# Cross-scan layers: the softplus's difference from GpSimd to VectorE, without ScalarE's pass that subtracts the one

## What is computed

```python
delta = jax.nn.softplus(delta + delta_bias[None, :, None])
def step(h, inp):
    dt, ut, bt, ct = inp
    dA = jnp.exp(dt[..., None] * A_k[None])
    dBu = dt[..., None] * bt[:, :, None, :] * ut[..., None]
    h = dA * h + dBu
    y = jnp.einsum('bkdn,bkn->bkd', h, ct)
    return (h, y)
```

## Time and profile before

| what | us |
|---|---|
| median of 3 runs | 3782.1 |
| fastest and slowest run | 3761.59 and 3788.62 |
| span of the profiled execution | 3763.2 |
| one image of the last layer, order-0 turn and order-1 turn | 182.4 and 169.2 |

### The profile page before, as it was taken

How to read it: one execution, slowest core, us unless ns; L and a number is a source line. 1 busy time by engine, 2 the same in 40 slices (tenths; PEclk the granted TensorE clock), 3 DMA queues, 4 the chain that set the end, 5 groups by cost and what they waited for, 6 DMA issues and landing times. The chain is left out here.

```text
span 3763.2 us, 27831 instructions
## 1 busy us (share of the span) xinstructions
PE 2803.9 (75%) x6084; PEld 631.1 (17%) x6084; DVE 3005.3 (80%) x1944; ACT 2039.5 (54%) x2278; POOL 2826.3 (75%) x1212
## 2 busy tenths in 40 slices
PE   5668777877887788345667677688878787877887
PEld 2111111111111111111111121111111111111111
DVE  1889898888889896676988824988889888889883
ACT  3566565656565664314555425656565556656562
POOL 1899899988999897003655515999889989989993
PEclk9788888778788878667889788778787878888788
DMA  2655646553755554103443305475555555564652
GB/s 59 156 124 137 147 124 159 127 132 98 164 129 140 126 142 101 28 2 89 119 102 86 100 3 124 108 168 131 130 125 136 136 126 136 134 139 122 156 126 56
DMA packets 140402, 437.16 MB, mean 116 GB/s; under 512 B 33429, under 2 KB 34139, under 8 KB 139915
## 3 DMA queue, kind: packets, MB, share of 16 engines
q1 hardware_dynamic: 140234, 435.53, 48.2%
HBM read 307.50 MB, written 6.82 MB: 84 GB/s over the span
## 5 line engine op out<-in xcount | busy, mean ns | idle before, releaser
L863 POOL TENSOR_TENSOR L_read<-L_state,L_c_rows 128x1024 f32<-128x1024 f32 x768 | 1800.6, 2363 | 206.7 <-PE L_y_ps L656 176.7
L656 PE MATMUL L_y_ps<-L_read,L_fold 128*64 128x512 f32 x3072 | 1256.5, 913 | 426.2 <-POOL L_read L863 390.0
L794 ACT ACTIVATE L_work_ps<-L_delta,L_a_neg 128x1024 f32<-128x1024 f32 x256 | 286.3, 1118 | 677.2 <-DVE L_state L971 677.2
L971 DVE TENSOR_TENSOR_SCAN L_state<-L_work_ps,L_state 128x1024 f32<-128x1024 f32 x256 | 583.7, 2280 | 80.4 <-POOL L_state L850 76.6
L850 POOL TENSOR_TENSOR L_state<-L_du,L_b_rows 128x1024 f32<-128x1024 f32 x256 | 606.0, 2367 | 25.1 <-POOL L_read L863 3.1
L971 DVE TENSOR_TENSOR_SCAN L_state<-L_decay,L_work_ps 128x1024 f32<-128x1024 f32 x256 | 585.3, 2286 | 29.9 <-DVE L_work_ps L952 6.8
L794 ACT ACTIVATE L_decay<-L_delta,L_a_neg 128x1024 f32<-128x1024 f32 x512 | 584.9, 1142 | 14.6 <-DVE L_state L971 11.3
L971 DVE TENSOR_TENSOR_SCAN L_state<-L_decay,L_row_ps 128x1024 f32<-128x1024 f32 x256 | 585.5, 2287 | 8.8
L952 DVE TENSOR_TENSOR L_work_ps<-L_du,L_row_ps 128x1024 f32<-128x1024 f32 x256 | 314.4, 1228 | 268.5 <-issue 143.2
L656 PEld LDWEIGHTS L_y_ps<-L_read,L_fold 128*64 128x64 f32 x3072 | 184.9, 159 | 1372.8 <-POOL L_read L863 976.4
L1501 POOL TENSOR_TENSOR L_read<-L_state,L_c_rows 128x1024 f32<-128x1024 f32 x96 | 235.5, 2458 | 189.7 <-PE L_y_ps L1297 106.4
(11 more groups left out here) (322 smaller groups left out, 2981.1 us busy)
## 6 DMA issues: line engine op xcount, KB each, us to landing
L_c_rows<-L_bc_dram SPq DMA_DIRECT2D x580, 256.0 KB, 4.0
L_b_rows<-L_bc_dram SPq DMA_DIRECT2D x580, 256.0 KB, 4.2
L_delta<-L_delta SPq DMA_DIRECT2D x204, 256.0 KB, 5.9
L_du<-L_du SPq DMA_DIRECT2D x140, 256.0 KB, 6.2
L_du<-L_u SPq DMA_DIRECT2D x64, 256.0 KB, 6.0
L_bc_dram<-L_dbl SPq DMA_DIRECT2D x40, 128.0 KB, 3.5
L_delta<-L_delta_a SPq DMA_DIRECT2D x16, 256.0 KB, 4.4
L_du<-L_du_a SPq DMA_DIRECT2D x16, 256.0 KB, 5.3
```

Of the source, the lines that this page charges most:

```text
L656: m = nc.tensor.matmul(y_ps[i * BLK:(i + 1) * BLK, c, :], fold[:, :], y_half(t, o, i), start=first, stop=last, skip_group_check=True)
L794: nc.scalar.activation(to[:, :], delta2[:, d * NBLK + c, :], ACT.Exp, scale=a_neg[:, o * 2 + d, c, p:p + 1]).then_inc(decay_ready, 1)
L863: nc.gpsimd.tensor_tensor(read[:, t % READS, :], state[:, t % STATES, :], c_rows[:, g % 2, :], ALU.mult).then_inc(multiplied, 1)
L971: nc.vector.tensor_tensor_scan(state[:, c, way], by[:, way], fed[:, way], 0.0, ALU.mult, ALU.add).then_inc(scanned, 1)
```

## The change

The gap moves from GpSimd's list to VectorE's. It is now one instruction that takes the rounded sum `more` = 1 + e as it is, adds -1 and subtracts l; ScalarE's "less" and its constant column go away, and the gap waits for "one" instead. A new table puts the gaps behind VectorE's scans of tiles 30, 38 and 41 in order 0 and of tiles 23, 29 and 35 in order 1. In the head, VectorE makes the three gaps before its first tile, and GpSimd forms du only. The conv-scan layer stays as it was.

```diff
-POOL_GAP = [{29: 0, 36: 1, 39: 2}, {22: 0, 28: 1, 34: 2}]
+DVE_GAP = [{30: 0, 38: 1, 41: 2}, {23: 0, 29: 1, 35: 2}]
...
                     if j > 0 or not isinstance(turn, Head):
                         act.wait_ge(sp_gap, n)
                     nc.scalar.activation(more[:, :], e[:, :], ACT.Identity, bias=1.0).then_inc(sp_one, 1)
-                elif kind == "less":
-                    act.wait_ge(sp_one, n + 1)
-                    nc.scalar.activation(more[:, :], more[:, :], ACT.Identity, bias=minus_col[:, :]).then_inc(sp_less, 1)
                 else:
                     act.wait_ge(sp_gap, n + 1)
                     nc.scalar.activation(l[:, :], l[:, :], ACT.Relu).then_inc(sp_relu, 1)
...
                         if at == t:
                             softplus(turn, kind, j)
 
-            ahead = {0: (("exp", 0), ("log", 0), ("one", 0), ("less", 0), ("exp", 1), ("log", 1), ("relu", 0), ("one", 1),
-                         ("less", 1)),
-                     1: (("exp", 2), ("log", 2), ("relu", 1), ("one", 2), ("less", 2)), 2: (("relu", 2),)}
+            ahead = {0: (("exp", 0), ("log", 0), ("one", 0), ("exp", 1), ("log", 1), ("relu", 0), ("one", 1)),
+                     1: (("exp", 2), ("log", 2), ("relu", 1), ("one", 2)), 2: (("relu", 2),)}
             for _, key, i in HEAD_SIDES:
                 if key[0] == "sum" and i == 0:
                     for kind, j in ahead[key[1]]:
...
 
         @block.gpsimd
         def _(pool):
-            def gap(turn, j):
-                n = turn.next * NJ + j
-                pool.wait_ge(sp_log, n + 1)
-                pool.wait_ge(sp_less, n + 1)
-                l = l_of[j]
-                nc.gpsimd.tensor_tensor(l[:, :], more[:, :], l[:, :], ALU.subtract).then_inc(sp_gap, 1)
-
             def add_x(turn):
 
                 wait_side(pool, turn.use(("out", 0), 1))
...
                                             ALU.mult).then_inc(multiplied, 1)
                     if turn.finish and t == ADD_AT:
                         add_x(turn)
-                    if t in POOL_GAP[turn.r]:
-                        gap(turn, POOL_GAP[turn.r][t])
 
             def form_du(j):
 
                 wait_side(pool, Head().use(("sum", j), 1))
                 nc.gpsimd.tensor_tensor(du[j], delta[:, j, :], u[:, j, :], ALU.mult).then_inc(sp_du, 1)
 
-            gap(Head(), 0)
-            gap(Head(), 1)
-            form_du(0)
-            gap(Head(), 2)
-            form_du(1)
-            form_du(2)
+            for j in range(NJ):
+                form_du(j)
             over_turns(pool, turn_of)
             add_x(Tail())
 
...
                     dve.wait_ge(rooted, done + 1)
                     nc.vector.tensor_tensor(sq_b[0:C, s], sq_a[0:C, s], side_ps[0:C, :], ALU.mult).then_inc(side_free, 1)
 
+            def gap(turn, j):
+
+                n = turn.next * NJ + j
+                dve.wait_ge(sp_log, n + 1)
+                dve.wait_ge(sp_one, n + 1)
+                l = l_of[j]
+                nc.vector.scalar_tensor_tensor(out=l[:, :], in0=more[:, :], scalar=-1.0, in1=l[:, :], op0=ALU.add,
+                                               op1=ALU.subtract).then_inc(sp_gap, 1)
+
             def inject_tile(number, t):
 
                 T, (d, p, c) = number * NT + t, tiles[t]
...
                     way = slice(None, None, 1 if d == 0 else -1)
                     nc.vector.tensor_tensor_scan(state[:, c, way], by[:, way], fed[:, way], 0.0, ALU.mult,
                                                  ALU.add).then_inc(scanned, 1)
-
+                    if t in DVE_GAP[turn.r]:
+                        gap(turn, DVE_GAP[turn.r][t])
+
+            for j in range(NJ):
+                gap(Head(), j)
             over_turns(dve, turn_of)
             for _, key, i in TAIL_SIDES:
                 if key[0] in ("cent", "shift", "out"):
```

More of the change, by code:

```diff
@@ L319 @@
             ("dt", 2): (22, 24), ("u", 2): (26, 27), ("sum", 0): (28, 29), ("sum", 1): (31, 32), ("sum", 2): (36, 37)}]
-ACT_SOFTPLUS = [{("exp", 0): 28, ("log", 0): 29, ("one", 0): 30, ("less", 0): 31, ("relu", 0): 33, ("exp", 1): 36,
-                 ("log", 1): 37, ("one", 1): 38, ("less", 1): 39, ("exp", 2): 39, ("log", 2): 40, ("relu", 1): 41,
-                 ("one", 2): 41, ("less", 2): 42, ("relu", 2): 44},
-                {("exp", 0): 21, ("log", 0): 22, ("one", 0): 23, ("less", 0): 24, ("relu", 0): 26, ("exp", 1): 27,
-                 ("log", 1): 28, ("one", 1): 29, ("less", 1): 30, ("relu", 1): 32, ("exp", 2): 33, ("log", 2): 34,
-                 ("one", 2): 35, ("less", 2): 36, ("relu", 2): 38}]
-POOL_GAP = [{29: 0, 36: 1, 39: 2}, {22: 0, 28: 1, 34: 2}]
+ACT_SOFTPLUS = [{("exp", 0): 28, ("log", 0): 29, ("one", 0): 30, ("relu", 0): 33, ("exp", 1): 36,
+                 ("log", 1): 37, ("one", 1): 38, ("exp", 2): 39, ("log", 2): 40, ("relu", 1): 41,
+                 ("one", 2): 41, ("relu", 2): 44},
+                {("exp", 0): 21, ("log", 0): 22, ("one", 0): 23, ("relu", 0): 26, ("exp", 1): 27,
+                 ("log", 1): 28, ("one", 1): 29, ("relu", 1): 32, ("exp", 2): 33, ("log", 2): 34,
+                 ("one", 2): 35, ("relu", 2): 38}]
+DVE_GAP = [{30: 0, 38: 1, 41: 2}, {23: 0, 29: 1, 35: 2}]
 ACT_SIDES = ("u", "bc", "dt", "sum", "z", "cent", "var")
@@ L410, in cross_scan_layer @@
         eps_col = sb("eps_col", [128, 1])
-        minus_col = sb("minus_col", [128, 1])
         w_u, w_z, w_bc_a, w_bc_b, w_dt = given.w_u, given.w_z, given.w_bc_a, given.w_bc_b, given.w_dt
@@ L439, in cross_scan_layer @@
         (set_up, consts, side_ready, side_free, sp_abs, sp_exp, sp_log, sp_one,
-         sp_less, sp_gap, sp_relu, sp_du, delta_ready, decay_ready, scanned, injected, injected_c, b_ready,
+         sp_gap, sp_relu, sp_du, delta_ready, decay_ready, scanned, injected, injected_c, b_ready,
          multiplied, y_added, bc_stored, y_free, y_out, rooted, silued, gated, x_added) = (
@@ L443, in cross_scan_layer @@
                 "set_up", "consts", "side_ready", "side_free", "sp_abs", "sp_exp", "sp_log",
-                "sp_one", "sp_less", "sp_gap", "sp_relu", "sp_du", "delta_ready", "decay_ready",
+                "sp_one", "sp_gap", "sp_relu", "sp_du", "delta_ready", "decay_ready",
                 "scanned", "injected", "injected_c", "b_ready", "multiplied", "y_added", "bc_stored", "y_free", "y_out", "rooted",
@@ L501, in cross_scan_layer @@
         tiles = [(d, p, c) for d in range(DIRS) for p in range(NP) for c in range(NBLK)]
-        n_setup = 4 + 1 + 2 + 4 + 4 + 2
+        n_setup = 3 + 1 + 2 + 4 + 4 + 2
         @block.sync
@@ L900, in _ @@
             setup(nc.vector.memset(eps_col[:, :], eps))
-            setup(nc.vector.memset(minus_col[:, :], -1.0))
             setup(nc.vector.tensor_tensor(fold[:, :], ident[:, 0:BLK], ident[:, BLK:128], ALU.add))
```

## The result

The changed kernel takes 3752.4 us, the kernel before 3772.7 (medians of 20 runs each). The ratio is 0.9944, 95% interval 0.993 to 0.9959: 20 us or 0.56% faster, inside the 1% that the prediction called the limit of a measurement, and inside its range. The median of three runs from which the forecast subtracted its 16 us stood 9 us above that of twenty.

A forecast was written before the change was run, and what follows sets the result against it. Neither GpSimd nor VectorE bounds alone; both are about nine tenths loaded and hand tiles to each other. Heads 3, order-0 turns 13, order-1 turns 0: 16 us off the 3782.1 median gives 3766, range 3722 to 3806.

The forecast's parts named there:

- Sum: Whole span: 3 us for heads, 13 for order-0 turns, 0 for order-1 turns, so 16 us faster.
- Heads: Two heads: removed pass and ScalarE's idling go, so TensorE's first sum starts 1.6 us earlier; 3 us together.
- Order-0 turns: Eight turns, places behind scans 30, 38, 41: between 0.3 us lost and 2.8 gained each; 1.6 taken, 13 in all.
- I take 1.6, between them: Gain per order-0 turn, chosen between 0.3 us lost and 2.8 gained, nearer to the one place followed, tile 38.
- Order-1 turns: Eight turns, places at tiles 23, 29, 35: VectorE's delay offsets GpSimd's gain; between 2.5 us lost and 2.8 gained, 0 taken.
- Collision: New VectorE instructions wait for GpSimd's running product, taking 1.2 to 3.4 us; about 48 products exceed 3 us, held 0.95.
- A: Rival: GpSimd sets the pace and keeps its gain at two of three places; 53 us plus heads' 3, 3726; chance 0.25.
- B: Rival: VectorE sets the pace, made late by collisions at 40 places; 40 us slower, 3822; chance 0.09.
- C: Rival: nothing is left, VectorE's delays match what GpSimd gains; 3782; chance 0.19.

The follow-up runs named there:

- the kernel with the pass alone: Kernel before with only ScalarE's subtracting pass removed, difference kept on GpSimd; taken from e: 3751.0 us, from the rounded sum: 3752.2 us.
- the second form of the pass alone: Kernel before without ScalarE's subtracting pass; GpSimd subtracts l from the rounded sum, ScalarE's relu takes the one off by its bias: 3752.2 us, ratio 0.9947.
- the kernel without collisions: Changed kernel whose new VectorE instruction reads a PSUM decay tile instead of the rounded sum at 40 places (delta differs): 3714.4 us, ratio 0.984.

## Why the prediction was right, and where its steps were not

**Sum.** 16 us forecast, 20 measured; the likeliest case. That the two lie so close is in good part luck: the three terms of the sum were 3 us for the heads, 13 for the order-0 turns and 0 for the order-1 turns, and only the second stands, with one half of its reason. What the runs show is one wait, for the removed pass at tile 38 of the order-0 turns, worth 18 us.

**Heads.** Expected 1.6 us each. Both first sums start 1.8 us earlier after the exponential. The last head ends 1.9 us earlier, but the first 0.6 later: there TensorE's first sum, pair by pair of matmuls, changed so; first before, then after:

```profile
73.00 2.08 PE L631 MATMUL L_side_ps<-L_y_a,ident 128*128 128x512 f32 x2 [7.58 <-ACT L_y_b L752]
74.87 1.77 PE L631 MATMUL L_side_ps<-L_y_b,L_minus_w 128*128 128x512 f32 x2
76.47 1.02 PE L631 MATMUL L_side_ps<-L_delta,ident 128*128 128x512 f32 x2
```

```profile
71.80 2.08 PE L630 MATMUL L_side_ps<-L_y_a,ident 128*128 128x512 f32 x2 [5.79 <-ACT L_y_b L748]
73.67 1.91 PE L630 MATMUL L_side_ps<-L_y_b,L_minus_w 128*128 128x512 f32 x2
75.38 1.91 PE L630 MATMUL L_side_ps<-L_delta,ident 128*128 128x512 f32 x2
```

The lower level lasted one pair longer. So 1.3 us in place of 3 in this execution, and even that is not the change's: the same heads in six kernels take 38.9 us on average (36.9 to 40.6), and before they took 38.8 and 38.9. In the kernel with the pass alone the sums start 1.1 us earlier and the heads take 41.5 and 41.1. The term left out the clock, and its 3 us are not shown.

**Order-0 turns.** Expected 1.6 each, measured 1.7 in six (inside the spread of single turns) and 5.1 in two. The size came from the right place for half of the reason. The wait for the removed pass, 1.48 at the one place that I followed, is what counts, and the run without the pass shows it at all eight; in the first turns it is 3.7 and in one more 3.2, which the prediction did not count. The other half, 1.4 us gained on GpSimd per place, came to nothing: 89 of GpSimd's 97 us are idle time now, and the change gains no more than the pass alone. What is late next is not VectorE's scans, as the prediction had it, but mostly TensorE's sums (75 us more waiting, against 13 for scans). By this the term "I take 1.6, between them" was a middle between two ends, and its landing on 1.7 proves little.

**Order-1 turns.** Expected 0, measured 0 in the six middle ones. The prediction had VectorE's lateness cancel GpSimd's gain along the way. In fact the turns are 2.2 us ahead until tile 36 and lose it at sum 2, by a relu that stands behind a decay; moving it kept the lead. The two last turns of a layer grew by 4.1 us, which was not foreseen. By the starts of GpSimd's reads 2.1 us of it is there at tile 15, ahead of the first moved instruction, and the second form of the pass alone, with nothing moved, shows 2.2 there, so that part is not the move's and stays open; 2.3 more come between tiles 36 and 38, where the middle turns lose their lead.

**Collision.** Durations from 1.20 to 3.40 with a mean of 1.97 us, close to the forecast. Of GpSimd's products 26 are over 3 us, not 48: at the others GpSimd waits for TensorE just then, and its next product is not held, or by 0.3 us at most. The hold is as taken, 28 products over 2.6 us by 25.4 us in all, 0.91 each.

**Rivals.** A's 56 us are near what the kernel without collisions reaches (58 us under before), but A had counted the held products in, so the agreement doesn't show A's mechanism. B had the mechanism but not the sum: 38 us are lost to the collision, against a gain of about the same size. C had the move's own balance, nothing left (3752.4 with it, 3752.2 without), and missed the pass.

## What to carry to other kernels

Before moving elementwise work from GpSimd to VectorE, look at where its operands are: two SBUF inputs beside a busy GpSimd cost more here than the rest of the instruction (38 us against about 14), and with one input in PSUM there was no collision. When a change does two things, run each alone: here deleting a pass that another engine waited for brought everything, and the larger move beside it added nothing: the wait that it takes away was gone already, and the collision ate the rest. A wait put into an engine's list is paid by all that stands behind it, so read that list down to the next copy that frees a buffer.

## What was not expected of the hardware

A collision is decided by hundredths of a microsecond. Two order-1 turns of the changed kernel at tile 23, GpSimd's products and the new instruction:

```profile
344.85 1.20 DVE L928 SCALAR_TENSOR_TENSOR L_y_b<-L_more,L_y_b 128x1024 f32<-128x1024 f32 x1
344.89 5.70 POOL L851 TENSOR_TENSOR L_read<-L_state,L_c_rows 128x1024 f32<-128x1024 f32 x2
...
690.77 4.68 POOL L851 TENSOR_TENSOR L_read<-L_state,L_c_rows 128x1024 f32<-128x1024 f32 x2
...
693.14 3.39 DVE L928 SCALAR_TENSOR_TENSOR L_y_b<-L_more,L_y_b 128x1024 f32<-128x1024 f32 x1
```

In the first VectorE starts 0.04 us before the product, takes 1.20, and two products take 5.70. In the second the pair takes 4.68 and its second product begins just ahead of VectorE's instruction, which takes 3.39.
